# A Macaron block with a mixture of experts: the gate multiply of the gathered results moves from ScalarE to VectorE

## The reference

```python
x = x + 0.5 * ffn(layernorm(x))
x = x + attn(layernorm(x))
x = x + 0.5 * ffn(layernorm(x))

def attn(x):                      # windows of 128 tokens, TOPK = 32
    q, k, v = xw @ Wq.T + bq, xw @ Wk.T + bk, xw @ Wv.T + bv
    scores = q @ k.T / sqrt(128)  # 128 x 128 in each window
    masked = scores where among the row's 32 largest, else -inf
    out = softmax(masked) @ v
    r = leaky_relu(out) + x
    return layernorm(r) * gamma + beta

def ffn(x):
    normed = layernorm(x) * ln_gamma + ln_beta
    top_v, top_i = top_k(softmax(normed @ router_w.T), 2)   # 2 of 8 experts
    gates = softmax(top_v)
    out = sum over the two chosen experts e of gates[e] * swiglu_e(normed)  # 128 -> 384 -> 128
    return out + swiglu_shared(normed)                      # 128 -> 128 -> 128
```

## Time and profile before

| | |
|---|---|
| median of 3 runs | 585.65 us (580.63 to 588.22) |
| the profiled execution | 585.65 us |
| its span | 583.9 us |
| mean granted clock of PE | 0.948 |
| busy: PE, DVE, ACT, POOL | 502.6, 369.6, 364.1, 324.2 us |
| DMA, mean over the span | 202 GB/s |

### The profile page before, as it was taken

One profiled execution on the slowest core, in us unless ns is written; L12 is line 12 of the kernel. 1 busy time (PEld: TensorE's weight loads), 2 busy tenths in 40 slices (PEclk: granted clock), 3 DMA queues, 4 the chain that ended last, 5 costly groups with the idle time before them and its releaser, 6 DMA issues.

```text
span 583.9 us, 14651 instructions
## 1 busy us (share of the span) xinstructions
PE 502.6 (86%) x3928; PEld 459.4 (79%) x3928; DVE 369.6 (63%) x1701; ACT 364.1 (62%) x914; POOL 324.2 (56%) x491
## 2 busy tenths in 40 slices
PE   2588999989998999999986599986999998999681
PEld 1466999989996999988964479774998998999670
DVE  5568874732548899859787869989884232232433
ACT  3386565574678787877855557845645546456662
POOL 2274777765574675447475305673677666565141
PEclk9999999999999999999987579997999999999795
DMA  6946667766785555674312345522668776777883
GB/s 180 309 121 204 201 226 251 253 234 239 256 295 180 193 193 192 243 258 171 119 47 68 118 163 183 176 74 100 220 220 265 253 242 224 281 248 235 253 281 104
DMA packets 88014, 117.84 MB, mean 202 GB/s; under 512 B 11848, under 2 KB 60880, under 8 KB 87936
## 3 DMA queue, kind: packets, MB, share of 16 engines
...
## 4 chain that ended last, share of the span: by engine, by line
PE 55%; ACT 13%; SPq 9%; issue 7%; DMA 6%; DVE 5%; POOL 3%; ACTq 1%; DVEq 0%; POOLq 0%
PE ps_y L730 13%; PE ps_g L716 12%; PE ps_h L721 6%; PE ps_u L721 6%; DMA xin<-rows 4%; SPq L441 3%; PE w L630 3%; PE ps_x L711 2%; ACT zz L849 2%; SPq L484 2%; ACT yg L909 2%; PE w L660 2%; SPq L479 2%; POOL rows L1567 2%; ACT L901 2%
## 5 line engine op out<-in xcount | busy, mean ns | idle before, releaser
L1584 POOL DMA_INDIRECT results<-raw_gu,idx x163 | 160.5, 985 | 159.7 <-ACT raw_gu L938 117.4
L1567 POOL DMA_INDIRECT rows<-zz,s_idx x128 | 125.5, 980 | 63.7 <-issue 29.6
L730 PE MATMUL ps_y<-dn_t,raw_gu 128*128 x978 | 140.4, 280 | 7.9 <-ACT raw_gu L938 6.6
L716 PE MATMUL ps_g<-x_t,raw_dn 128*128 128x128 f32 x978 | 138.4, 278 | 0.0
L730 PEld LDWEIGHTS ps_y<-dn_t,raw_gu 128*128 128x128 f32 x978 | 124.1, 194 | 15.0 <-issue 14.4
L716 PEld LDWEIGHTS ps_g<-x_t,raw_dn 128*128 128x128 f32 x978 | 123.9, 194 | 2.5 <-issue 2.3
L938 ACT COPY raw_gu<-ps_y 128x128 f32<-128x128 f32 x163 | 43.0, 264 | 93.9 <-PE ps_y L730 92.3
L1394 DVE TENSOR_TENSOR raw_gu<-sil,ps_u 128x384 f32<-128x384 f32 x82 | 45.1, 550 | 71.7 <-PE ps_u L721 49.2
L932 ACT ACTIVATE sil<-ps_g 128x384 f32<-128x384 f32 x163 | 80.3, 492 | 16.1 <-PE ps_g L716 15.0
L929 ACT ACTIVATE x_t<-ps_x,bf_c,gf_c 128x128 f32<-128x128 f32 x163 | 75.4, 463 | 13.1 <-PE ps_x L711 13.1
L1394 DVE TENSOR_TENSOR raw_gu<-sil,ps_h 128x384 f32<-128x384 f32 x81 | 44.6, 550 | 46.1 <-PE ps_h L721 33.7
...
## 6 DMA issues: line engine op xcount, KB each, us to landing
raw_dn<-gu_t SPq DMA_DIRECT2D x163, 384.0 KB
xin<-rows SPq DMA_DIRECT2D x163, 64.5 KB
yg<-results SPq DMA_DIRECT2D x15, 512.0 KB, 4.7
results<-raw_gu,idx POOLq DMA_INDIRECT x163
...
rows<-zz,s_idx POOLq DMA_INDIRECT x128
...
```

The costliest lines, as they stand in the source:

```text
L716: t = pe.matmul(ps_g[k][:, c, :], ws[:, k4, c * P:(c + 1) * P], x_t[:, k, :], start=True, stop=True)
L730: t = pe.matmul(ps_y[:, 0, :], h_t[:, k4, c * P:(c + 1) * P], dn[:, bass.ds(off + c * D, D)], start=(c == 0), stop=(c == FC - 1))
L1567: pool.indirect_dma_start(xs, bass.IndirectOffsetOnAxis(s_idx[n][:, c, k:k + 1], 0), zz[n][:, k, c, :], None).then_inc(scat[n], 16)
L1584: pool.indirect_dma_start(yt, bass.IndirectOffsetOnAxis(idx[:, ky:ky + 1], 0), yb[:, ky, :], None).then_inc(yst[ky], 16)
```

## The change

The multiplication by the gates goes from ACT to DVE. `gated` and its calls are removed, and with them ACT's waits for the load (`yld`) and for the gates (`gts`), and the semaphore `yw_done`. `combine` on DVE now waits for the load itself, multiplies all 1024 numbers of a partition by the gates in one tensor_tensor with a broadcast operand (L1279 in the changed kernel, in place), and then makes the two adds as before (now L1284). Since `cb` now counts three instructions in a combine, its constants go from 2 to 3. After the multiply there is one more `turn()`, and the ones in `gated` are gone, so the table `WEAVE` was made anew for all five engines: the same blocks are worked, but their parts stand at other places between the attention and the routing.

```diff
 WEAVE = {
     "sp": """
-        10 7 2 7 7 4 6 10 22 14 12 34 12 4 19 11 36 12 6 z1 25 12 37 5 z2 5 z2 1 6 z6""",
+        9 7 4 6 3 11 3 8 24 12 9 39 10 5 20 6 32 20 7 z1 14 22 37 2 5 z1 3 z1 1 2 5 z6""",
...
-        yw_done = sem("yw_done")
...
-                   (nm_done, 1), (o_ps, 1), (o_sb, 1), (v_sb, 1), (x2_done, TB), (cb, 2 * 2)]
+                   (nm_done, 1), (o_ps, 1), (o_sb, 1), (v_sb, 1), (x2_done, TB), (cb, 2 * 3)]
...
-        N_CB = 2
+        N_CB = 3
...
-            def gated(C, n, tile):
-
-                act.wait_ge(yld[n], (C - n) * 8 + 16)
-                for c in range(2):
-                    for k in range(TB):
-                        t = act.activation(yg[n][:, k, c, :], yg[n][:, k, c, :], ACT.Copy, scale=gates[:, c, tile + k:tile + k + 1])
-                    t.then_inc(yw_done, 1)
-                    turn()
-
...
-            act.wait_ge(gts, 1)
             for s, f in enumerate(TURNS):
                 a, A, J, p = f[:4]
                 if a in ALONE:
-                    gated(a, a % 2, a * TB)
                     norm_x(a, chain_alone[a])
...
-                if p is not None:
-                    gated(p, p % 2, p * TB)
                 if a is not None:
                     scores(a)
...
             gates_of_layer(1)
-            act.wait_ge(gts, 2)
-            for J in range(PHASE[-1].lo):
-                gated(STEPS + J, J % 2, J * TB)
             turn.rest()
...
             def combine(C, n, tile):
 
+                dve.wait_ge(yld[n], (C - n) * 8 + 16)
+                of = gates[:, :, tile:tile + TB].rearrange("p c (t o) -> p t c o", o=1).broadcast_to([P, TB, 2, D])
+                dve.tensor_tensor(yg[n][:], yg[n][:], of, ALU.mult).then_inc(cb, 1)
+                turn()
                 xr = xres[:, tile:tile + TB, :]
                 for c in range(2):
-                    dve.wait_ge(yw_done, C * 2 + c + 1)
-                    if c:
-                        dve.wait_ge(cb, C * N_CB + 2 * N_CB + 1)
+                    dve.wait_ge(cb, C * N_CB + 2 * N_CB + c + 1)
                     dve.tensor_tensor(xr, xr, yg[n][:, :, c, :], ALU.add).then_inc(cb, 1)
                     turn()
```

More of the change, by code:

```diff
@@ L114 @@
     "sp": """
[L115 removed]
+        9 7 4 6 3 11 3 8 24 12 9 39 10 5 20 6 32 20 7 z1 14 22 37 2 5 z1 3 z1 1 2 5 z6""",
     "pe": """
[L117 to L118 removed]
+        z5 2 2 z1 1 z1 3 z1 1 z2 2 4 2 z1 4 2 4 6 z2 4 2 4 z1 3 2 3 7 z1 7 6 2 2 6 1 92 3 z1 3 z1 14 3 z1 3 4 4 6 8 4 3 2 7 3 4 6 4 4 12 2 21 3 z1 3
@@ L119 @@
+        z1 4 5 5 z1 2 1 z1 6 7 z1 5 2 4 4 1 z1 1 z2 1 z7 1 3 z2 3 7 z1 6 z1 5 9 4 1 z2 1 3 9 z1 5 z1 2 4 z3 6 z1 5 z1 12 3 4 5 z1 20 3 6 4 z1 79""",
     "act": """
[L120 to L122 removed]
+        z12 1 1 z3 2 1 3 z5 1 1 z3 1 z1 7 2 1 z3 2 4 2 1 z4 7 z3 4 z2 10 1 3 9 4 59 1 z2 3 3 z1 2 7 z2 1 2 4 z4 1 2 2 1 9 z2 1 1 5 z2 1 z2 7 z1 2 4
@@ L123 @@
+        z2 2 3 2 4 z1 1 z2 21 z2 1 2 1 2 2 1 3 z1 2 z4 1 z1 2 z1 2 z1 2 4 2 z3 6 3 2 3 z4 1 z5 1 z1 1 z15 1 z1 2 z2 2 z1 1 z2 8 1 6 5 z8 1 2 1 z1 2
+        2 2 z2 4 1 5 1 z6 2 1 z2 6 z1 5 z3 2 3 4 14 z1 1 z1 2 5 1 40 15 78""",
     "dve": """
-        z153 1 z1 1 z4 1 z22 1 z1 1 z12 1 z2 1 z7 1 z6 1 z8 1 z3 1 z8 1 z1 1 2 z2 1 z19 1 1 z2 1 z7 2 z4 1 6 6 1 1 1 z2 1 z8 2 z2 3 z8 1 z6 1 z10 1
-        z1 1 z12 1 z5 1 1 z4 1 z2 1 z10 2 z10 1 z6 1 z12 1 z3 2 z12 1 z7 1 1 z18 1 z7 1 z2 1 z13 1 z1 1 1 z6 1 z6 4 z17 1 z5 2 z20 1 z1 1 z7 1 z20 1
@@ L126 @@
-        z2 1 1 z4 1 z5 1 z27 1 z104 2 z17 1 z6 1 z1 1 z7 1 z6 1 z4 1 z5 1 z28 2 z16 1 z1 1 z20 1 z10 2 z52 1 z23 1 z2 1 z8 1 z4 1 z15 1 1 z24 1 1
-        z15 1 z6 1 z13 1 z1 2 2 z24 1 z1 2 3 1 1 1 z3 1 z1 1 3 2 z1 1 z1 8 5 z2 1 z1 2 3 z3 1 1 1 1 2 z1 1 3 z4""",
+        z153 2 z9 1 z17 1 z9 1 z3 1 z5 1 z9 1 z6 1 z10 1 1 z11 2 z1 2 z12 1 1 z6 1 z8 1 z5 1 z2 13 z1 3 1 z2 1 z8 1 z1 1 z1 1 z1 1 z5 2 z8 1 z11 1
+        z8 1 1 z5 1 1 z7 2 z7 1 z2 1 z24 1 z5 1 z6 1 z1 1 z9 2 z5 1 z2 1 z22 1 z6 1 z12 2 z5 1 1 z3 1 z10 1 1 z5 1 z4 1 z8 2 z9 1 z7 1 z17 2 z12 1
@@ L128 @@
+        z9 1 z1 2 z8 1 z28 1 z106 2 z19 1 z5 1 z1 1 z3 1 z4 1 z10 1 z2 1 z24 2 z20 1 z4 1 z21 1 2 z61 1 z23 1 z1 1 z9 1 z3 1 z11 1 z19 1 z10 1 1 z18
+        1 z2 1 z9 1 1 z3 1 z2 1 z19 1 z5 1 1 z9 1 1 z2 9 z2 3 2 z2 6 z2 10 z1 1 z1 3 z4 1 z1 2 1 z1 2 2 z6""",
     "pool": """
-        z20 2 1 z2 1 z3 4 z2 1 1 3 z2 1 6 z1 1 1 z1 6 2 1 z2 1 1 1 5 5 3 7 18 9 3 z1 2 3 z1 5 z2 7 3 1 z1 4 z1 6 13 19 z2 2 z1 5 3 6 z2 4 z3 3 z11 7
-        1 4 3 z1 5 1 z1 4 z4 6 z4 3 z1 2 2 4 1 z1 5 1 z1 7 2 1 z2 5 4 2 z1 9 7 1 5 2 4 4 9 29""",
+        z20 2 1 z2 1 z1 1 z4 7 z1 2 5 z2 1 2 1 6 z1 3 z2 1 z1 4 z1 1 2 z1 7 z1 19 13 2 2 6 2 3 2 z1 1 6 2 3 1 z2 5 29 1 2 2 2 4 4 z1 3 3 z1 3 z2 1 2
@@ L131 @@
+        z11 4 5 7 z1 2 1 1 1 2 2 z3 6 z4 4 z1 1 1 1 2 3 5 1 2 4 3 z3 4 7 z3 6 11 1 10 3 9 z1 19""",
 }
```

## The result

The changed kernel took 589.14 us in the median of 20 runs (582.93 to 593.31), against 585.37 us for the kernel before in as many (580.63 to 590.02): a ratio of 1.0054, with a 95% interval from 1.0034 to 1.0076. That is about 3 us slower, where I had forecast 5.4 us faster. The profiled execution took 590.26 us, its span 588.5. The ratio leaves out the few runs that lie over 1.5% above the fastest of their kernel. Single runs of one kernel scatter over some 10 us here, so a trace tells where time went, and only the ratios tell how much.

What follows compares the result with a forecast made beforehand. PE was taken to set the pace over most of the run, DVE during attention and routing; −1.5 − 0.5 − 1.1 + 1.0 + 0 − 1.3 − 2.0 = −5.4 from 585.65 gave 580 us (576 to 584; 8-in-10 range 568 to 593).

Steps and rivals of the forecast that it cites:

- Step (1): PE-bound first layer, combines 0 to 2: relieving ACT closes PE gaps at 185 to 190 us; −1.5 us.
- Step (3): Combine 4, near 255 us: adds end earlier and DVE's attention chain passes the time on; −1.1 us.
- Step (2): Near the end of the PE-bound first layer: one pair of table loads less on ACT; −0.5 us.
- Step (4): Combines 3, 5, 7: multiplies replace shorter waits, +1.0 us; combine 6: multiply hidden by a wait for logits, 0.
- Step (5): Restart at 404 us: ACT does x_t and sil before the exponentials, saving a table load; −1.3 us.
- Step (6): Last 52 us: PE gaps of 4.56 and 1.56 us go, a 4.3 us load stall comes; −2 us.
- the first rival: All waits for ACT go and DVE never stands in front of a load: 570.6 us, chance 0.22.
- The second: Rival: nothing visible, PE-bound stretches hide ACT's relief and multiplies replace waits on DVE; 586 us, chance 0.19.
- The third: Rival: slower, in the tail DVE waits for loads with h queued behind; 593.6 us, chance 0.15.

Runs made afterwards that it cites:

- e1: Multiply on DVE in all combines, block order of the kernel before kept, against the kernel before: 583.87 us, ratio 0.9952.
- h3: e1 with attention step 3 alone in the new order: 584.09 us, ratio 0.9952 to the kernel before.
- h1: g2 with five expert-block parts on PE moved ahead of the projection of v in attention step 3: 582.08 us, ratio 0.9931 to the kernel before.
- h4: e1 with attention step 4 alone in the new order: 587.42 us, ratio 1.0039 to the kernel before.
- f2: e1 with attention steps 0 to 2 in the new order: 585.76 us, ratio 0.9982 to the kernel before.
- g2: e1 with the new order from attention step 5 on, tail included: 582.24 us, ratio 0.9920 to the kernel before.
- e2: Changed kernel with the old order up to the first attention step: 588.63 us, ratio 1.0054 to the kernel before.
- f1: Changed kernel with attention step 3 in the old order on all five engines: 587.91 us, ratio 1.0013 to the kernel before.
- i1: e1 with the new order of attention step 4 on DVE alone: 586.61 us, ratio 0.9970 to the kernel before.
- i2: e1 with the new order of attention step 4 on PE alone: 586.52 us, ratio 0.9994 to the kernel before.
- f3: e1 without the fifteen multiplies, a maximum over 8 numbers in their place, so different output: 580.02 us, ratio 0.9890 to the kernel before.
- g3: e1 with the multiply on DVE only in combines 0 to 7, on ACT in the tail: 584.72 us, ratio 0.9979 to the kernel before.
- g4: e1 with the multiply on DVE only in the tail's seven combines, on ACT before: 584.73 us, ratio 0.9958 to the kernel before.

## Why the prediction was wrong

I forecast 5.4 us faster, and the kernel became 3 us slower. What failed is the sum as a whole in one respect, that it has no term for the new order of the blocks away from a combine, a table load or the restart, and its steps (1) and (3).

**The mechanism of the multiply was right, and it is a gain.** Its price was 1.22 us forecast and 1.222 measured. By itself it makes the kernel 0.5% faster (e1), about 2.8 us. DVE's waits name the load where they named ACT, 13.4 us in all (10.1 in e1).

**Step (1) failed.** I took −1.5 us for ACT's relief at 185 to 190 us. In the windows of e1 and of the changed kernel this stretch reads:

```profile
185.00:190.00 5.00, 3.46 (x32) 3.23 (x31) 3.50 (x12) 4.87 (x10) 2.09 (x2) 1.00 0.61 226
```

```profile
185.00:190.00 5.00, 5.00 (x47) 5.00 (x46) 3.46 (x12) 4.96 (x10) 2.69 (x5) 1.00 0.57 201
```

In e1 ACT is still busy 4.87 of 5.00 without any gating, and PE's gap is 1.54 where it was 1.96: 0.4 us came back and not 1.5. With the new order PE is full there, but it has a gap elsewhere: between 200 and 220 us it is busy 17.75 us of 20, before it was busy all 20. A stretch in which an engine is full says that it is full, not of what.

**Step (3) failed in the words "DVE carries the attention chain, so the time is passed on".** In the changed kernel combine 4 ended 3.2 us earlier, not 1.1. But this lead is the new order's and not the multiply's: in e1 the multiply stands behind the h that waits 2.87 us for u, begins at 255.89, and the adds end at 258.6, where they ended before. And the lead isn't passed on. In DVE's queue the bias add of `v` stands within the search, it needs `v` from PE, and PE brings it when it always did. h3 has the lead and is as fast as e1; h1 has the parts ahead of `v` and is as fast as g2. DVE was busy 4.96 of 5.00 in one window, and I read this as "DVE is the chain". The chain went through PE and ACT at several places in each step.

**What was left out of the sum cost most.** I priced the new order at the places that the order shows near a combine, a table load or a restart, and took all others as neutral without a reason. The 1.0% between e1 and the changed kernel, 6 us, is the order alone. Of it, step 4 is 5 us by the ratios (h4 against e1, give or take 2.4), more than the whole gain of the multiply; its trace accounts for 2.3 us up to the list, and where the rest arises stays open; step 3 is nothing (h3); steps 0 to 2 cost about 0.3% (f2, not clear of noise); from step 5 on it gives perhaps 0.3% back (g2). The start costs nothing at the end (e2). These add up to less than the whole by some 0.2%, which the intervals allow. That f1 came out 0.4% under the changed kernel while h3 equals e1 stays open; the intervals of f1 and the changed kernel overlap. In step 4 the traces of i1 and i2 show two places that lengthen the way to the list: an h ahead of the statistics on DVE, and a down projection moved behind the transposes of `xn` on PE. What each is worth at the end isn't shown. Both could be read in the order before the run; I hadn't looked there.

**Step (2)** is not seen: f2 has the 26 table loads of the changed kernel in the old order of the rest, and is not faster than e1 with 28 (0.9982 against 0.9952). **Step (4)** came to nothing: from the first round of the search of step 2 to the list of the second layer e1 takes 99.2 us and the kernel before 99.6, and from there to the fourth list 116.2 and 115.8, so multiplies and waits balance. f3's list comes at 316.4 us, 2.1 us ahead of e1's, but that isn't the multiplies: g3 has them all in this phase, has the full clock at the logits as f3 has, and writes the list at 316.2. **Step (5)** had the right size: from the list ahead of it to the first transpose of the next blocks the changed kernel takes 18.5 us, before 19.4, and the transpose waits for nothing:

```profile
408.85 0.42 PE L710 MATMUL ps_x<-ident,xin 128*128 128x128 f32 x1
```

That is −0.9, forecast −1.3. But the same order has a price ahead of it: between the first two lists of the second layer e2, f1, g2 and h1, which have it, take 68.1 to 68.4 us, and the kernels with the old order 65.9 to 66.9 (the changed kernel itself 65.5). **Step (6)** had the right size: −2.0 us forecast, and g4, which does this alone (in the old order), has 0.9958, about 2.5 us. In the changed kernel the gap of 4.56 us is gone; the stall of 4.20 on DVE is there, and PE waits 1.05 of it. In g4 the two gaps of 4.56 and 1.56 us are gone too, but PE waits 1.24 us for an h and longer for rows (2.34 and 3.17 us, before 1.04 and 1.39). No term of the sum had these, so its size was met partly by luck.

**The range** had a slip of its own: the ends given with the six steps do not add up to 576 to 584. The low ends come to 570.6, as in the first rival, and the high ends, with the −2 of step (6), to 588.9, close to what was measured.

**The rivals.** The first (all waits for ACT go, 570.6) was too low, since there was less on the path than the waits add up to. The second (nothing, 586) is where the multiply and the order together nearly ended; but it is the difference of two effects and no "nothing". The third (h held behind a load, 593.6) names the right queue at the wrong place: in the tail PE has a cover, in step 4 an h ahead of the statistics did cost, for want of u and not of a load. Its test, a slower g4, came out the other way (0.9958), and so did g2, which has the new order of the tail (0.9920).
